# A fused attention and expert kernel: the order of steps inside a batch is changed

## The chip, the cores and the metric

The kernel runs on one core of a Trainium2 chip (trn2). The metric is the device time of one execution in microseconds (us), the median of the runs shown. The engines are called TensorE (PE), VectorE (DVE), ScalarE (ACT), GpSimd (POOL) and SyncE (SP); SP issues most of the DMAs here.

## The reference, cut to what matters

The input is 16 batches of 512 rows of 256 float32 numbers. Each row is normalised, and two branches of the normalised rows are added to the input.

```python
xn = layernorm(x)                                  # 16 x 512 x 256
x = x + attn(xn) + ffn(xn)

# attn: 16 heads of 16 columns, q and k through low-rank factors
q = (xn @ q_a) @ q_b;  k = (xn @ k_a) @ k_b;  v = xn @ v_w.T + v_b
att = softmax(where(causal, q k^T / sqrt(16), min))
y = (att @ v) @ o_w.T + o_b

# ffn: 8 experts, each takes the 128 rows of a batch with the highest probability
probs = softmax(xn @ choice_w.T)
G, I = top_k(probs transposed, 128)
out[I] += G * (silu(xn[I] @ w1) @ w2)
```

## The kernel before

The attention part comes first, and the experts after it. The change touches the attention part alone.

**Groups, slots and units.** A batch's 16 heads are worked on in four groups of four heads, so there are 64 groups, numbered n = 4 b + g. The attention part is a sequence of slots, one for each group: slot (b, g) has the number G = 4 b + g. A slot has ten units (`UN`). In every unit TensorE computes two tiles of 128 x 512 scores. The first, `scoret`, holds the transposed scores of group G + 1; ScalarE takes its exponential, and GpSimd sets the part above the diagonal to zero (L887, L565, L469). The second, `score`, holds the scores of group G + 3; VectorE takes its row maxima (L866, L719), which the later `scoret` of the same group subtracts. A `score` tile has three PSUM banks in turn, so the score of unit u waits until VectorE has finished that of unit u - 3; `scoret` has two banks, and waits for the exponential of unit u - 2.

**Steps between the units.** All other work is cut into steps, which `slot_steps` (L53) puts behind the units of a slot. Two tables by g say where: an entry (t, kind, ahead, k) stands behind unit t. `SUMS` holds the steps of a group: `pv` (probabilities times values, four steps; the last is followed by ScalarE's copy `yraw`), `maxt` and `maxd` (the row maxima are transposed, and written by a small DMA of ScalarE's queue into row KS of `qstk`), and `ytr` (transposing y back and dividing it by the denominator). `PROJECTIONS` holds the steps of a batch, for the batch b + ahead:

- `xload`: SP loads the rows of batch b + 2 into `xln` (L382). It waits only until the rows before it are normalised.
- `lnstat` (two halves), `lnapply`: VectorE takes mean and variance, GpSimd takes the power -1/2, VectorE writes `xn`, and SP stores it.
- `xt` (two): TensorE transposes `xn`, ScalarE and VectorE split it in a high and a low part.
- `qk_first` and `qk` (k = 0 to 3): three matmuls each of 128 x 512, the two halves of one tile of queries or keys. k = 0, 1 are queries, k = 2, 3 keys. ScalarE takes the high part (L537), and VectorE the rest (L588).
- `mid` (k = 0 to 3): ScalarE takes the middle part of a tile (L541), GpSimd the low one (L460). Behind k = 1 SP issues six DMAs of 256 KB that write the queries into `qstk`, and behind k = 3 six that write the keys into `kstk` (L393 to L400).
- `v` (four): the values and the router's logits of the next batch. `yt` (two), `o` (four): the output projection of the batch before. `xres`: loading of the input rows that the output is added to (L406), and GpSimd's addition of the bias (L477).

The first `score` of batch b + 1 stands in unit 0 of slot (b, 1), and waits for all twelve of those DMAs:

```python
if g == 0 and k == 0:
    pe.wait_ge(stacked[b % 2], at(STACK_DMAS * (b // 2 + 1), STACK_DMAS))
```

The keys of batch b + 1 are written behind `mid` k = 3 in slot (b, 0), the slot right before.

**What sets the order.** Every engine walks through the same list of steps and takes its own part of each, in the list's order, and SP its DMAs. The steps of the kinds in `shared` use two PSUM banks in turn, in the order of the list (`unit_of`). The whole order is thus the two tables. The 16 batches are run as eight pairs: the first and the last pair are written out, and pairs 1 to 6 are the body of a loop (`eng.Fori(1, PAIRS - 1)`, L342) which each engine runs by itself. Its back branch comes before the batches 4, 6, 8, 10 and 12. Those five are called the batches behind the branch here; 1, 2, 3, 5, 7, 9, 11, 13 and 14 are the nine others in whose slot 0 the keys of the next batch are written.

Of the kernel before, what the change touches and what calls it, by code (L numbers as in the profile page):

```python
# [25 lines left out]
def unit_parts(t, transposed):  # L26
# [5 lines left out]
    for h, i in parts:  # L32
# [4 lines left out]


PROJECTIONS = (
# [5 lines left out]
     (9, "qk_first", 2, 1)],  # L45
    [(0, "qk", 2, 1), (0, "mid", 2, 0), (1, "mid", 2, 1), (4, "qk_first", 2, 2), (6, "qk", 2, 2), (8, "mid", 2, 2),
     (8, "qk_first", 2, 3), (9, "qk", 2, 3)])

SUMS = (
# [4 lines left out]


def slot_steps(b, g):
# [1125 lines left out]
```

## Time and profile before

| what | value |
|---|---|
| median of 3 runs | 1301.05 us (1294.84 to 1301.11) |
| profiled execution, its own time | 1295.71 us |
| its span, first to last instruction | 1293.8 us |
| TensorE busy | 1184.1 us, 92% |
| VectorE busy | 967.2 us, 75% |
| ScalarE busy | 668.7 us, 52% |
| GpSimd busy | 692.0 us, 53% |

The page of the profile gives busy times by engine, the busy share in 40 slices of the span, and the costliest groups. Views of the trace give the same by stretch (windows), who waited for whom (waits), and the instructions of an engine in order of time (timeline). Times in them count from the start of the span. A matmul's duration in them covers its whole way through the array, so matmuls that follow each other overlap; what one costs is the distance to the next start.

### The profile page before, as it was taken

What the parts mean: (1) busy time and instruction counts of PE and PEld (TensorE: products, weight loads), DVE (VectorE), ACT (ScalarE), POOL (GpSimd) and SP (SyncE); (2) the same over time, 40 slices, a digit from 0 to 9 for tenths busy, and PEclk for the clock granted to TensorE, in tenths of its full rate; (3) what the DMA queues carried; (4) which work ended last, traced back from release to release, by engine and by line L of the source; (5) the groups of instructions that cost most, each with busy time, mean ns of one, the idle gap of its engine ahead of it and who ended that gap; (6) DMA issues with size and microseconds to landing.
All of it is one profiled execution on the core that took longest, in us unless ns stands there. A gap on an engine that the chain in (4) does not pass through costs nothing. (4 is left out here: it accounts for less than half of the span.)

```text
span 1293.8 us, 29459 instructions
## 1 busy us (share of the span) xinstructions
PE 1184.1 (92%) x8502; PEld 819.8 (63%) x8502; DVE 967.2 (75%) x3293; ACT 668.7 (52%) x1312; POOL 692.0 (53%) x1021
## 2 busy tenths in 40 slices
PE   6799999999999999999999998769999999999995
PEld 5545555555555555555555553348988888888885
DVE  3588888879889888888888879935666666666662
ACT  2357667667667677677667665522332323233320
POOL 1235344355355355345345443344888888888885
PEclk9779999999999999999999999979999999999998
DMA  5443443443443443443444342132555555556454
GB/s 141 114 116 83 116 116 100 116 116 98 115 115 98 115 115 99 115 115 100 113 115 112 100 99 67 34 114 38 111 99 95 114 93 102 94 100 109 85 78 53
DMA packets 106287, 130.31 MB, mean 101 GB/s; under 512 B 21580, under 2 KB 75476, under 8 KB 106196
## 3 DMA queue, kind: packets, MB, share of 16 engines
q1 hardware_dynamic: 76356, 94.46, 28.1%
q0 software_dynamic: 24576, 33.57, 15.6%
q10 hardware_dynamic: 5264, 1.32, 0.5%
q8 instruction: 27, 0.44, 0.1%
q14 instruction: 64, 0.52, 0.1%
HBM read 44.84 MB, written 33.55 MB: 61 GB/s over the span
## 5 line engine op out<-in xcount | busy, mean ns | idle before, releaser
L719 DVE CUSTOM_DVE_ANT_0 junk<-bank,rowmask 128x256 bf16<-128x256 f32 (+3 forms) x1024 | 454.9, 485 | 60.3 <-PE bank L866 38.0
L565 ACT ACTIVATE probs<-bank 128x512 f32<-128x512 f32 x640 | 377.3, 598 | 158.0 <-PE bank L887 143.8
L469 POOL TENSOR_SCALAR_AFFINE_SELECT probs<-probs 128x256 f32<-128x256 f32 (+1 forms) x640 | 224.2, 363 | 311.0 <-ACT probs L565 308.9
L866 PE MATMUL bank<-kstk,qstk 96*128 96x256 bf16 (+3 forms) x1024 | 250.7, 306 | 34.3 <-DVE rowmax L719 17.3
L887 PE MATMUL bank<-qstk,kstk 98*128 98x256 bf16 (+3 forms) x1024 | 251.0, 307 | 3.8 <-ACT probs L565 2.6
L1049 POOL DMA_INDIRECT out_rows<-mixed,rows x128 | 208.9, 1632 | 58.2 <-issue 38.1
L1078 ACT ACTIVATE hid<-bank 128x512 f32<-128x512 f32 x128 | 76.6, 598 | 228.5 <-PE bank L1141 228.5
L908 PE MATMUL bank<-probs,vaug 128*32 128x512 f32 (+3 forms) x2048 | 168.5, 448 | 6.6 <-POOL probs L469 6.6
L1157 PE MATMUL bank<-w_hi,hid_hi 128*128 128x256 f32 x512 | 147.3, 288 | 0.0
L1157 PE MATMUL bank<-w_hi,hid_lo 128*128 128x256 f32 x512 | 144.9, 283 | 0.0
L1157 PE MATMUL bank<-w_lo,hid_hi 128*128 128x256 f32 x512 | 144.8, 283 | 0.0
L866 PEld LDWEIGHTS bank<-kstk,qstk 96*128 96x128 bf16 x1024 | 89.7, 100 | 79.5 <-DVE rowmax L719 38.3
L887 PEld LDWEIGHTS bank<-qstk,kstk 98*128 98x128 bf16 x1024 | 76.7, 99 | 99.2 <-issue 48.0
L1109 DVE TENSOR_SCALAR mixed<-bank,gate_sel 128x256 f32<-128x256 f32 x128 | 56.1, 480 | 92.0 <-PE bank L1157 92.0
L908 PEld LDWEIGHTS bank<-probs,vaug 128*32 128x32 f32 x2048 | 54.1, 110 | 95.9 <-issue 74.1
L460 POOL TENSOR_TENSOR qk_part<-rest,qk_part 128x512 bf16<-128x512 f32 x64 | 74.6, 1166 | 58.0 <-ACT qk_part L541 55.1
L1157 PEld LDWEIGHTS bank<-w_lo,hid_hi 128*128 128x128 f32 x512 | 98.2, 192 | 0.0
L1157 PEld LDWEIGHTS bank<-w_hi,hid_hi 128*128 128x128 f32 x512 | 98.2, 192 | 0.0
L1157 PEld LDWEIGHTS bank<-w_hi,hid_lo 128*128 128x128 f32 x512 | 98.1, 192 | 0.0
L1098 DVE CAST hid_hi<-hid 128x512 fp32r<-128x512 f32 x128 | 56.9, 445 | 48.7 <-ACT hid L1078 47.1
L1100 DVE TENSOR_TENSOR hid_lo<-hid,hid_hi 128x512 fp32r<-128x512 f32 x128 | 89.2, 697 | 4.4
L719 DVE DVE_READ_ACCUMULATOR2_ANT rowmax<- 128x1 f32 x1024 | 84.8, 83 | 0.0
(131 smaller groups left out, 2097.8 us busy)
## 6 DMA issues: line engine op xcount, KB each, us to landing
qstk<-qk_part SPq DMA_DIRECT2D x96, 256.0 KB, 4.8
kstk<-qk_part SPq DMA_DIRECT2D x96, 256.0 KB, 4.7
xln<-in_L_attn_hidden_states SPq DMA_DIRECT2D x16, 512.0 KB, 6.1
xn_rows<-xn SPq DMA_DIRECT2D x16, 512.0 KB, 2.8
xres<-in_L_attn_hidden_states SPq DMA_DIRECT2D x16, 512.0 KB, 3.6
out_rows<-xres SPq DMA_DIRECT2D x16, 512.0 KB, 2.9
qstk<-in_L_ffn_w SPq DMA_DIRECT2D x8, 512.0 KB, 4.0
kstk<-in_L_ffn_w SPq DMA_DIRECT2D x8, 512.0 KB, 3.9
```

What stands on the lines that cost most here:

```text
L460: nc.gpsimd.tensor_tensor(qk_part[2][:, k, :], rest[k % 2][:], qk_part[1][:, k, :], ALU.subtract).then_inc(lo_done, 1)
L469: nc.gpsimd.affine_select(out=block, in_=block, compare_op=ALU.is_ge, fill=0.0, base=0, pattern=[[0, len(cols)], [1, P]], channel_multipli ...
L565: nc.scalar.activation(probs[n % 2][:, 512 * k:512 * k + 512], SCORET[k % 2][:], ACT.Exp, scale=SCALE).then_inc(exp_done, 1)
L719: last = nc.vector.tensor_tensor_reduce(out=junk[k % 2][:, col:col + width], in0=SCORE[score_bank(UN * n + k)][:, col:col + width], in1=ro ...
L866: last = nc.tensor.matmul(SCORE[score_bank(UN * n + k)][:, col:col + width], qstk[b % 2][0:KS, GH * g + h, P * i:P * i + P], kstk[b % 2][0 ...
L887: last = nc.tensor.matmul(SCORET[k % 2][:, col:col + width], kstk[b % 2][0:KS + SHIFT, GH * g + h, P * j:P * j + P], qstk[b % 2][0:KS + SH ...
L908: last = nc.tensor.matmul(Y[2 * HD * h:2 * HD * h + 2 * HD, P * k:T], vaug[b % 2][:, k, GH * g + h, :], probs[n % 2][:, col:col + width], ...
L1049: nc.gpsimd.indirect_dma_start(out=out_rows, out_offset=bass.IndirectOffsetOnAxis(ap=moe.rows[:, GB4 * grp + j, e:e + 1], axis=0), in_=mix ...
L1078: nc.scalar.activation(hid[k % 2][:], UP[k][:], ACT.Silu).then_inc(silu_done, 1)
L1098: nc.vector.tensor_copy(hid_hi[n % 2][:, k, :], hid[k % 2][:]).then_inc(hid_high, 1)
L1100: nc.vector.tensor_tensor(hid_lo[n % 2][:, k, :], hid[k % 2][:], hid_hi[n % 2][:, k, :], ALU.subtract).then_inc(hid_done, 1)
L1157: last = nc.tensor.matmul(DOWN[k][:, D * t:D * t + D], a, b, start=m == 0, stop=m == len(todo_mm) - 1)
```

## The change

The tables `PROJECTIONS` and `SUMS` are replaced, and nothing else. No step is added or removed. In `PROJECTIONS`, `xload` goes from unit 2 to unit 0 of slot 0; `lnstat` from (slot 0, unit 9) and (slot 1, unit 1) to units 5 and 9 of slot 0; `lnapply` from unit 5 to unit 2 of slot 1. `v` 0 leaves unit 0 of slot 0, and `v` 1, `v` 2 and `o` 0 stand in a group at unit 9 of slot 0; `v` 3 goes from unit 0 to unit 9 of slot 1. `yt` 0 goes from unit 1 to 0, `xres` from unit 1 to unit 9 of slot 2. `qk` 0, `qk_first` 1 and `qk` 1 stand in a group at unit 0 of slot 3; `mid` 0, 1 and 3 come one to two units later. In `SUMS`, `maxt`, `maxd`, `pv` 2 and `pv` 3 get places that differ by slot.

```diff
 PROJECTIONS = (
-    [(0, "v", 1, 0), (1, "mid", 1, 3), (1, "yt", -1, 0), (2, "xload", 2, 0), (6, "yt", -1, 1), (8, "v", 1, 1),
-     (9, "lnstat", 2, 0), (9, "v", 1, 2)],
-    [(0, "v", 1, 3), (1, "lnstat", 2, 1), (2, "o", -1, 0), (5, "lnapply", 2, 0), (5, "o", -1, 1), (6, "o", -1, 2),
-     (8, "o", -1, 3)],
-    [(0, "xt", 2, 0), (1, "xres", 0, 0), (1, "xt", 2, 1), (6, "qk_first", 2, 0), (8, "qk", 2, 0),
-     (9, "qk_first", 2, 1)],
-    [(0, "qk", 2, 1), (0, "mid", 2, 0), (1, "mid", 2, 1), (4, "qk_first", 2, 2), (6, "qk", 2, 2), (8, "mid", 2, 2),
-     (8, "qk_first", 2, 3), (9, "qk", 2, 3)])
+    [(0, "xload", 2, 0), (0, "yt", -1, 0), (2, "mid", 1, 3), (5, "lnstat", 2, 0), (6, "yt", -1, 1), (8, "v", 1, 0), (9, "v", 1, 1), (9, "v", 1, 2), (9, "lnstat", 2, 1), (9, "o", -1, 0)],
+    [(2, "lnapply", 2, 0), (6, "o", -1, 1), (6, "o", -1, 2), (8, "o", -1, 3), (9, "v", 1, 3)],
+    [(0, "xt", 2, 0), (1, "xt", 2, 1), (8, "qk_first", 2, 0), (9, "xres", 0, 0)],
+    [(0, "qk", 2, 0), (0, "qk_first", 2, 1), (0, "qk", 2, 1), (2, "mid", 2, 0), (3, "mid", 2, 1), (6, "qk_first", 2, 2), (8, "qk", 2, 2), (9, "mid", 2, 2), (9, "qk_first", 2, 3), (9, "qk", 2, 3)])

 SUMS = (
-    [(2, "pv", 0, 0), (2, "pv", 0, 1), (3, "maxt", 2, 0), (4, "maxd", 2, 0), (5, "pv", 0, 2), (5, "pv", 0, 3), (7, "ytr", 0, 0)],
...
+    [(2, "pv", 0, 0), (2, "pv", 0, 1), (4, "maxt", 2, 0), (5, "maxd", 2, 0), (5, "pv", 0, 2), (6, "pv", 0, 3), (7, "ytr", 0, 0)],
+    [(2, "pv", 0, 0), (2, "pv", 0, 1), (3, "pv", 0, 2), (3, "maxt", 2, 0), (4, "maxd", 2, 0), (5, "pv", 0, 3), (7, "ytr", 0, 0)],
+    [(2, "pv", 0, 0), (2, "pv", 0, 1), (2, "maxt", 2, 0), (2, "pv", 0, 2), (2, "maxd", 2, 0), (5, "pv", 0, 3), (7, "ytr", 0, 0)],
+    [(2, "pv", 0, 0), (2, "pv", 0, 1), (4, "maxt", 2, 0), (4, "pv", 0, 2), (5, "maxd", 2, 0), (5, "pv", 0, 3), (7, "ytr", 0, 0)])
```

The removed rows of `SUMS` are four times the one shown.

## Rows read from the trace of the kernel before

**Rows 1.** The page: TensorE's busy time, busy tenths, granted clock.

```profile
PE 1184.1 (92%) x8502; PEld 819.8 (63%) x8502; DVE 967.2 (75%) x3293; ACT 668.7 (52%) x1312; POOL 692.0 (53%) x1021
...
PE   6799999999999999999999998769999999999995
...
PEclk9779999999999999999999999979999999999998
```

**Rows 2.** Windows, slots of batches 7 and 8: length, then busy us by engine.

```profile
417.65:429.23 11.58, 11.46 (x97) 7.03 (x96) 10.08 (x40) 9.00 (x20) 4.77 (x12) 1.00 0.71 159
429.23:442.49 13.26, 11.75 (x101) 7.78 (x100) 10.90 (x50) 6.67 (x16) 4.75 (x12) 1.00 0.30 89
442.49:453.59 11.10, 11.02 (x89) 6.24 (x87) 10.14 (x42) 8.26 (x16) 4.02 (x6) 1.00 0.30 95
453.59:465.41 11.82, 11.74 (x85) 6.17 (x85) 9.88 (x40) 9.18 (x18) 8.35 (x19) 1.00 0.45 105
465.41:478.62 13.21, 11.80 (x96) 7.11 (x96) 9.81 (x40) 9.16 (x20) 4.77 (x12) 1.00 0.73 170
478.62:490.30 11.68, 11.68 (x101) 7.69 (x100) 10.77 (x50) 6.66 (x16) 4.71 (x12) 1.00 0.19 66
...
sum 95.65, PE 92.22 PEld 54.42 DVE 81.72 ACT 66.30 POOL 43.75; mean PE 11.53 PEld 6.80 DVE 10.22 ACT 8.29 POOL 5.47
```

**Rows 3.** Waits, whole span: us in total, times, longest.

```profile
PE bank L866 <- DVE rowmax L719: 17.3, 32, 1.3
...
DVE junk L719 <- issue: 15.2, 6, 3.0
...
PE bank L866 <- DMA kstk<-qk_part: 15.1, 9, 2.1
```

**Rows 4.** Timeline of TensorE around the slot change of batch 7.

```profile
428.38 0.39 PE L769 MATMUL bank<-wv_hi,xt_hi 128*128 128x264 f32 x1
...
429.23 0.39 PE L887 MATMUL bank<-qstk,kstk 98*128 98x512 bf16 x1
431.13 0.39 PE L866 MATMUL bank<-kstk,qstk 96*128 96x512 bf16 x1 [1.51 <-DMA kstk<-qk_part]
```

**Rows 5.** Timeline of ScalarE in batch 7, slot 0: its part of `mid` 3.

```profile
419.96 0.64 ACT L541 ACTIVATE qk_part<-rest 128x512 bf16<-128x512 f32 x1
```

**Rows 6.** Timeline of SP in 408 to 427 (start, us, line, tiles, count).

```profile
411.08 4.08 SPq L400 DMA_DIRECT2D qstk<-qk_part  x6
421.88 3.81 SPq L400 DMA_DIRECT2D kstk<-qk_part  x6
425.96 0.61 SPq L382 DMA_DIRECT2D xln<-in_L_attn_hidden_states  x1
```

**Rows 7.** Timeline of VectorE across the loop's branch, batch 8.

```profile
466.46 0.69 DVE L588 TENSOR_TENSOR rest<-bank,qk_part 128x512 f32<-128x512 f32 x1
470.13 0.69 DVE L719 CUSTOM_DVE_ANT_0 junk<-bank,rowmask 128x512 bf16<-128x512 f32 x1 [2.98 <-issue]
```

**Rows 8.** Timeline of TensorE in batch 8, slot 0: scores of units 3 and 5.

```profile
470.89 0.39 PE L866 MATMUL bank<-kstk,qstk 96*128 96x512 bf16 x1 [0.63 <-DVE rowmax L719]
...
472.87 0.39 PE L866 MATMUL bank<-kstk,qstk 96*128 96x512 bf16 x1 [0.66 <-DVE rowmax L719]
```

**Rows 9.** Timeline of TensorE: an `o` step and what follows it.

```profile
441.45 0.28 PE L769 MATMUL bank<-wo_lo,yt_hi 128*128 128x256 f32 x1
...
442.04 0.39 PE L887 MATMUL bank<-qstk,kstk 98*128 98x384 bf16 x2
```

**Rows 10.** The page, costliest groups: ScalarE's exponentials.

```profile
L565 ACT ACTIVATE probs<-bank 128x512 f32<-128x512 f32 x640 | 377.3, 598 | 158.0 <-PE bank L887 143.8
```

**Rows 11.** Line L400 in 421 to 426 (keys): issue to landing.

```profile
DMA to landing us min/median/max: 3.2/4.6/6.0
```

**Rows 12.** Line L400 in 410 to 416 (queries): issue to landing.

```profile
DMA to landing us min/median/max: 3.4/4.6/5.8
```

**Rows 13.** A window of VectorE's pause in batch 8 (last columns: clock, DMA share, GB/s).

```profile
467.50:469.70 2.20, 2.20 (x24) 0.90 (x22) 0.00 (x0) 1.84 (x4) 1.57 (x3) 1.00 0.01 6
```

3 rows, old and new, of the table SUMS are left out of this document.

## The prediction

> **What bounds the kernel now.** I read the page first: TensorE is busy 92% of the span, and in nearly every slice of the attention part the tenths say 9 or more at a granted clock of 9 tenths or more [rows 1]. Then one pair of batches by slots [rows 2]: TensorE is busy 92.22 of 95.65 us, VectorE 81.72, ScalarE 66.30. Every slot but two is TensorE's full time to within 0.12 us; the exceptions are slot 1 of batch 7 (13.26 long, 11.75 busy) and slot 0 of batch 8 (13.21 long, 11.80 busy). So the order of steps can give back only what TensorE idles, and the list of waits names both pieces [rows 3]: nine waits for the keys' DMAs, 15.1 us in all, and 17.3 us for VectorE's row maxima, which go with six pauses of VectorE that nothing releases (15.2 us, up to 3.0).
>
> *The keys.* In batch 7 TensorE issues the transposed score of slot 1 at 429.23, and the first score of the next batch only at 431.13 [rows 4], 1.90 later. The nine batches without the branch have this wait once each, and 15.1 / 9 = 1.68 of the 1.90 is the wait; the other 0.22 is the ordinary distance. The chain behind it, counted from the start of slot 0 at 417.65 [rows 2]: ScalarE's part of `mid` 3 at +2.31 [rows 5], GpSimd's behind it, SP's first issue at +4.23 [rows 6], the score at +13.48 [rows 4]. The DMAs alone are 9.25 us of that.
>
> *The branch.* In batch 8 VectorE issues the rest of `qk` 3 at 466.46 (+1.05 in the slot) and its next work at 470.13 (+4.72), idle for 2.98 us [rows 7]. TensorE meets this at the score of unit 3 (+5.48) and of unit 5 (+7.46) [rows 8]. The slot is 13.21 long where batch 7's takes 11.58 [rows 2], so 1.63 us are passed on. In return slot 1 of batch 8 doesn't wait for keys (11.68 against 13.26): the two losses cover each other, and a pair's two halves come out alike, 24.84 and 24.89 us for slots 0 and 1.
>
> **The change part by part.** No work is added, so TensorE's busy time stays, and only the two waits and new ones count.
>
> *o 0 into slot 0, v 0 and v 3 to the ends of their slots.* An `o` step costs 0.80 us (its last five matmuls take 442.04 - 441.45 = 0.59 [rows 9], the first some 0.2 more), a `v` 0.85 (428.38 to 429.23 [rows 4]). Slot 0 keeps its three `v` and gains `o` 0; slot 1 loses it. In a batch without the branch TensorE arrives at the first score of slot 1 at 11.58 + 0.23 + 0.80 = +12.6 instead of +11.8.
>
> *mid 3 from unit 1 to unit 2.* It now stands behind the exponential of unit 2 on ScalarE and the masking of unit 2 on GpSimd. With `v` 0 gone, ScalarE has one exponential of 0.60 [rows 10] more and the copies of `v` less in front of it, and must wait for unit 2's tile, which TensorE issues at about +1.4. I take +2.7 for ScalarE's part, 0.4 later than now, and the same 0.4 at SP: first issue at +4.63. Bounds: 0 (the `v` copies pay for it) and +1.2 (the whole distance of a unit, a tenth of 11.58). The keys then land for a score at 4.63 + 9.25 = +13.9, still behind TensorE's +12.6. So the wait stays at 1.3 us, and the slot change comes 0.4 later. What follows in slot 1 is 442.49 - 431.13 = 11.36 now and 10.56 without `o` 0. Slots 0 and 1: 13.9 + 10.56 = 24.4 against 24.84, a gain of 0.4 in each of nine batches.
>
> *xload to unit 0.* SP reaches it right behind the queries' DMAs, whose issue starts, with `mid` 1 two units later behind a group of three `qk` steps, some 8.5 us into slot 3, against 411.08 now. Rows and queries are then written by about +5.7 of slot 0, about when VectorE comes to `lnstat`, and before the keys' first packets. At present the load is issued behind the keys, at 425.96 [rows 6], and has nothing in front of it to gain from: the slowest DMA of the keys takes 6.0 us with the load behind it [rows 11], that of the queries 5.8 without [rows 12]. I count nothing for it; bounds: 0.2 us a batch won, and 2.4 lost if the rows, 512 KB, are still in front of the keys (256 KB take (9.25 - 3.2) / 5 = 1.2). The Trainium skill would allow more: "DMA: Bandwidth & Descriptors", "Issuing engines are not separate DMA queues", says that all DMAs run on the same 16 engines and interleave. By it the load could have slowed the keys, and its removal would give about a microsecond; the rows show 0.2.
>
> *The branch with v 0 gone.* VectorE is pinned: the rest of `qk` 3 still ends slot 3, so it restarts at +4.72, and what it does up to the score of unit 2 is the same. TensorE's score of unit 5 stays at +7.46 whatever TensorE does before, since it waits for unit 2's maxima. But `v` 0, which stood before that point, under the pause, now stands behind it, and so does `o` 0. From that score to the slot's end it is 478.62 - 472.87 = 5.75 us now, and 5.75 + 0.85 + 0.80 = 7.40 then, with 0.1 for `v` 0 waiting for a bank behind two more operations of VectorE (`lnstat` at unit 5): slot 0 takes 14.96 instead of 13.21, +1.75. Slot 1 loses `o` 0 (-0.80), and has three units without filler at its start, where the third transposed score waits for the first exponential: two units every 1.25 us by the 0.60 of an exponential [rows 10] and what I put around it, 0.35 more than the 0.90 of four tiles of 0.22. Slot 0 and 1: +1.3. Bounds: +0.8 (no new small wait, a fifth less passed on) and +2.3.
>
> *Slots 2 and 3.* `qk` 0, `qk_first` 1 move from slot 2 (11.10) to slot 3 (11.82) [rows 2], 1.5 us from one to the other and no change of their sum. Slot 2 falls to 9.6 us, for which VectorE has 10.14 - 0.69 = 9.45 us of work [rows 2, 7]: tight, but it carries up to two score tiles over. Small waits on VectorE go there (the list has 32, of 0.54 on average [rows 3]; I take 0.45 for the two slots), one of 0.35 for the exponential comes: -0.1. Bounds -0.5 and +0.8 (VectorE's deficit not carried). The pieces of `SUMS` move `pv` 2, `pv` 3 and `maxt` by a unit or two at the same cost; `xres`, eight units later, spares GpSimd a wait for its load, off the path.
>
> *The sum.* Nine batches x (-0.4 - 0.1) = -4.5. Five batches x (+1.3 - 0.1) = +6.0. Together +1.5 us: 1295.7 of the profiled execution becomes 1297.2. The median of the runs shown is 5.3 above that execution, and the same difference on it gives 1302.5; I put 1302.
>
> **The rivals.**
>
> 1. *The wait for the keys goes* (chance 0.28). If `mid` 3 is no later and TensorE's added 0.8 us fills the wait, nine batches win 0.8 + 0.1, with a shorter way of the keys up to the whole 1.67; with the branch at +0.6 in five: -9 x 1.3 + 5 x 0.6 = -8.7, 1292. For it: the way from ScalarE to SP has idle stretches. Against it: 9.25 of 13.48 us are DMAs that the change doesn't touch.
> 2. *VectorE's restart gets later* (chance 0.23), slower. The queries are issued 3 us later in slot 3 and the rows right behind them, so the DMA engines are at work while VectorE fetches what stands behind the branch; now they are nearly idle then, share 0.01 [rows 13]. The place is slot 0 of five batches, each us of the pause is passed on whole, and it decides from about 0.7 us on. With 1.5 us more, and the rows delaying the keys by 0.5 in nine batches: 5 x (1.2 + 1.5) + 9 x (-0.5 + 0.5) = +13.5, 1314. The Trainium skill speaks for the mechanism: "Runtime: NRT & Kernel Launch", "Instruction fetch mechanics", says that a taken branch outside the fetched window forces a DMA fetch before execution goes on. The trace's 2.98 us pause agrees.
> 3. *VectorE bounds slots 0 and 2* (chance 0.07): all of `lnstat` stands in slot 0 now, and slot 2 of 9.6 is shorter than VectorE's mean time in a slot, 81.72 / 8 = 10.2 [rows 2]. If nothing is carried over, 14 batches lose 0.6: 14 x 0.6 + 1.5 = +9.9, 1311.
>
> **How the numbers follow.** The forecast has the remaining chance, 0.42, with its own range of 1296 to 1308. A measurement of this kernel can tell 0.5%, 6.5 us, from no change. Faster by more than that: most of rival 1, and a little of the forecast, 0.27. Slower by more: rival 2 and most of 3, and the upper end of the branch's bound, 0.31. The rest, 0.42, is no change. The range reaches into rivals 1 and 2: 1288 to 1314.
>
> **What would show it.** The profile after should have slot 0 of a batch without the branch ending with `v`, `v`, `o` and then still a wait for the keys of about 1.3 us, SP's first key issue 4.6 us into the slot, and slots 0 and 1 together 24.4 us. Behind the branch slot 0 should take 15 us, VectorE's pause still 3.0, and slots 0 and 1 together 26.1. Slots 2 and 3 should be near 9.7 and 13.2. The forecast is wrong if the waits for the keys fall far below 9 x 1.3 us, if VectorE's pause changes, or if slot 2 is longer than 10.2.

## The result, and the profile after

| kernel | median | against before |
|---|---|---|
| before, beside it on the same chip | 1297.9 us (1293.5 to 1301.1) | |
| changed | 1321.6 us (1318.8 to 1323.4) | 1.018 [1.014, 1.023] |

The change makes the kernel slower by 1.8%, where the prediction said no change. The profiled execution of the changed kernel has a span of 1320.3 us, 26.5 more than before. Line numbers are four lower than before (L866 is L862, L887 L883, L719 L715, L400 L396, L382 L378).

The page of the changed kernel, its busy times, TensorE's busy tenths and the granted clock, to be held against [rows 1]:

```profile
PE 1191.3 (90%) x8502; PEld 822.0 (62%) x8502; DVE 1000.7 (76%) x3293; ACT 670.6 (51%) x1312; POOL 698.7 (53%) x1021
...
PE   6799999989989989989989997858999999999995
...
PEclk9779999989989989989989999978999999999998
```

Before, the nines ran through. Now an 8 comes back every three slices, some 100 us, the length of a loop pass, and the clock is 8 in the same slices. The windows of the slots of batches 7 and 8 in the changed kernel show where (columns as in [rows 2]; the third last is the clock):

```profile
426.72:439.55 12.83, 12.68 (x102) 7.71 (x102) 12.35 (x49) 9.88 (x23) 5.89 (x12) 1.00 0.94 215
439.55:450.78 11.23, 10.87 (x95) 6.75 (x94) 9.95 (x43) 6.52 (x12) 4.46 (x12) 1.00 0.14 48
450.78:460.56 9.78, 9.30 (x82) 5.33 (x81) 8.39 (x37) 7.04 (x16) 3.58 (x10) 1.00 0.32 108
460.56:474.09 13.53, 12.98 (x93) 7.32 (x91) 12.66 (x44) 9.84 (x19) 8.49 (x14) 1.00 0.28 69
474.09:495.36 21.27, 16.04 (x103) 9.12 (x102) 12.78 (x49) 10.05 (x23) 5.89 (x12) 0.76 0.54 131
495.36:506.24 10.88, 10.85 (x95) 6.69 (x94) 9.93 (x43) 6.51 (x12) 4.36 (x12) 1.00 0.14 49
```

One slot stands out: slot 0 of batch 8, the first behind the loop's back branch, takes 21.27 us where it took 13.21 [rows 2]. TensorE is idle for 5.2 of it, and its clock is 0.76 in the mean. Everything else is near the forecast.

From the starts of the batches (the distance from one batch's first transposed score to the next batch's) the difference of 26.5 us adds up:

| part | before | after | sum of the difference |
|---|---|---|---|
| five batches behind the branch | 47.8 to 47.9 | 54.8 to 55.9 | +37.0 |
| batches 7, 9, 11, 13 | 47.7 to 47.8 | 47.4 to 47.5 | -1.4 |
| batches 1, 2, 3, 5 | 48.2 to 50.0 | 47.4 to 47.7 | -6.5 |
| start, batches 0 and 14, all behind | | | -2.6 |

The waits of the whole span, to be held against [rows 3]:

```profile
PE bank L862 <- DVE rowmax L715: 41.6, 40, 5.0
...
DVE junk L715 <- issue: 28.8, 6, 5.8
...
PE bank L862 <- DMA kstk<-qk_part: 6.4, 10, 2.1
```

The wait for the keys fell from 15.1 to 6.4 us. But VectorE's pauses that nothing releases grew from 15.2 to 28.8 us, still six of them, and TensorE's waits for the row maxima from 17.3 to 41.6. The timeline of VectorE over the branch in batch 8, whose slot 0 starts at 474.09:

```profile
475.85 0.69 DVE L584 TENSOR_TENSOR rest<-bank,qk_part 128x512 f32<-128x512 f32 x1
482.23 0.69 DVE L715 CUSTOM_DVE_ANT_0 junk<-bank,rowmask 128x512 bf16<-128x512 f32 x1 [5.70 <-issue]
```

The rest of `qk` 3 is issued 1.76 us into the slot (before 1.05), the next work at +8.14 (before +4.72, [rows 7]): the pause is 5.70 us instead of 2.98. TensorE's score of unit 3 waits through it:

```profile
482.99 0.61 PE L862 MATMUL bank<-kstk,qstk 96*128 96x512 bf16 x1 [4.99 <-DVE rowmax L715]
...
485.44 0.63 PE L862 MATMUL bank<-kstk,qstk 96*128 96x512 bf16 x1
```

What SP issues around the branch, and what the DMA engines and the clock do then (timeline of SP; windows of 1 us with all engines):

```profile
469.18 3.80 SPq L396 DMA_DIRECT2D qstk<-qk_part  x6
473.78 0.39 SPq L378 DMA_DIRECT2D xln<-in_L_attn_hidden_states  x1
478.70 4.18 SPq L396 DMA_DIRECT2D kstk<-qk_part  x6
```

```profile
477.09:478.09 1.00, 0.91 (x9) 0.10 (x1) 0.00 (x0) 0.31 (x2) 0.89 (x2) 1.00 1.08 269
478.09:479.09 1.00, 0.00 (x0) 0.00 (x0) 0.00 (x0) 0.55 (x1) 0.87 (x2) 1.00 0.68 214
479.09:480.09 1.00, 0.00 (x0) 0.00 (x0) 0.00 (x0) 0.00 (x0) 0.01 (x1) 1.00 0.21 62
480.09:481.09 1.00, 0.00 (x0) 0.00 (x0) 0.00 (x0) 0.00 (x0) 0.00 (x0) 1.00 0.96 272
481.09:482.09 1.00, 0.00 (x0) 0.00 (x0) 0.00 (x0) 0.00 (x0) 0.00 (x0) 0.60 1.08 266
482.09:483.09 1.00, 0.10 (x1) 0.11 (x2) 0.86 (x3) 0.00 (x0) 0.00 (x0) 0.50 1.05 236
...
490.09:491.09 1.00, 1.00 (x7) 0.97 (x5) 0.74 (x2) 0.72 (x2) 0.12 (x1) 0.50 0.00 0
491.09:492.09 1.00, 1.00 (x7) 0.67 (x6) 0.88 (x6) 0.32 (x1) 0.29 (x1) 0.78 0.03 8
492.09:493.09 1.00, 1.00 (x10) 0.82 (x10) 0.96 (x3) 0.53 (x3) 0.29 (x1) 1.00 0.00 0
```

VectorE meets its branch at 475.94, and the queries and rows (2 MB in SP's queue) keep the DMA engines full until 478 and the last of them busy until 479.8, where before they were nearly idle [rows 13]. TensorE, with no `v` 0 to do, stands still for four whole windows; in the fourth of them its granted clock falls, and stays at 0.50, the lower of its two levels (1.2 GHz), until 491, 8 us after TensorE has work again.

One kind of packet tells when VectorE can go on. The DMA queue that the profile calls `instruction` carries one packet of 8 KB behind each of VectorE's branches. The DMA view of a window of 0.2 us around it, in the changed kernel (479.70 to 479.90, 3.84 us behind the branch) and in the one before (467.70 to 467.90, 1.2 us behind it):

```profile
q14 instruction: 1, 0.01, 9.7%
```

```profile
q14 instruction: 1, 0.01, 10.8%
```

In both, VectorE's next work starts 2.4 us after this packet, and in both the packet starts within 0.05 us of the last one of the queries and rows that stood queued. Few of the 16 DMA engines are still busy then. In the 0.9 us before it (478.90 to 479.78, changed kernel) the queries and rows fill 8.8% of the 16 engines, that is one or two of them; and an instruction packet at 473.60 starts while they are full (473.50 to 473.70):

```profile
q1 hardware_dynamic: 28, 0.03, 8.8%
```

```profile
q1 hardware_dynamic: 29, 0.05, 114.5%
q14 instruction: 1, 0.01, 18.9%
```

So the packet behind the branch seems to stand in line on one engine, the one that ends last.

### The profile page after: what moved, and what is told of

It reads as the page before. It is cut to its first block and busy times, and to the rows that moved or that the text cites. A ratio compares the mean times of both kernels' runs of the same rounds, so it can differ in the third digit from the quotient of the medians.

```text
span 1320.3 us, 29425 instructions
## 1 busy us (share of the span) xinstructions
PE 1191.3 (90%) x8502; PEld 822.0 (62%) x8502; DVE 1000.7 (76%) x3293; ACT 670.6 (51%) x1312; POOL 698.7 (53%) x1021
## 3 DMA queue, kind: packets, MB, share of 16 engines
q0 software_dynamic: 24576, 33.57, 15.1%
## 5 line engine op out<-in xcount | busy, mean ns | idle before, releaser
L715 DVE CUSTOM_DVE_ANT_0 junk<-bank,rowmask 128x256 bf16<-128x256 f32 (+3 forms) x1024 | 450.7, 485 | 78.5 <-PE bank L862 37.0
L561 ACT ACTIVATE probs<-bank 128x512 f32<-128x512 f32 x640 | 370.9, 599 | 175.0 <-PE bank L883 169.4
L465 POOL TENSOR_SCALAR_AFFINE_SELECT probs<-probs 128x256 f32<-128x256 f32 (+1 forms) x640 | 231.6, 364 | 402.0 <-ACT probs L561 396.1
L862 PE MATMUL bank<-kstk,qstk 96*128 96x256 bf16 (+3 forms) x1024 | 255.3, 311 | 49.0 <-DVE rowmax L715 41.6
L883 PE MATMUL bank<-qstk,kstk 98*128 98x256 bf16 (+3 forms) x1024 | 254.4, 311 | 10.5 <-ACT probs L561 8.8
L904 PE MATMUL bank<-probs,vaug 128*32 128x512 f32 (+3 forms) x2048 | 179.4, 451 | 1.3 <-POOL probs L465 1.3
L883 PEld LDWEIGHTS bank<-qstk,kstk 98*128 98x128 bf16 x1024 | 82.2, 99 | 133.7 <-issue 61.1
L862 PEld LDWEIGHTS bank<-kstk,qstk 96*128 96x128 bf16 x1024 | 89.3, 100 | 93.6 <-DVE rowmax L715 63.3
L904 PEld LDWEIGHTS bank<-probs,vaug 128*32 128x32 f32 x2048 | 49.9, 110 | 94.8 <-issue 90.3
L1137 PE MATMUL bank<-pt_hi,w_hi 128*128 128x512 f32 x256 | 81.6, 401 | 4.9 <-DVE pt_lo L1090 4.9
```

Of the source, the lines that this page charges most:

```text
L465: nc.gpsimd.affine_select(out=block, in_=block, compare_op=ALU.is_ge, fill=0.0, base=0, pattern=[[0, len(cols)], [1, P]], channel_multipli ...
L561: nc.scalar.activation(probs[n % 2][:, 512 * k:512 * k + 512], SCORET[k % 2][:], ACT.Exp, scale=SCALE).then_inc(exp_done, 1)
L715: last = nc.vector.tensor_tensor_reduce(out=junk[k % 2][:, col:col + width], in0=SCORE[score_bank(UN * n + k)][:, col:col + width], in1=ro ...
L862: last = nc.tensor.matmul(SCORE[score_bank(UN * n + k)][:, col:col + width], qstk[b % 2][0:KS, GH * g + h, P * i:P * i + P], kstk[b % 2][0 ...
L883: last = nc.tensor.matmul(SCORET[k % 2][:, col:col + width], kstk[b % 2][0:KS + SHIFT, GH * g + h, P * j:P * j + P], qstk[b % 2][0:KS + SH ...
L904: last = nc.tensor.matmul(Y[2 * HD * h:2 * HD * h + 2 * HD, P * k:T], vaug[b % 2][:, k, GH * g + h, :], probs[n % 2][:, col:col + width], ...
```

## The experiments

Each has its ratio to the kernel before, run on the same chip. "Branch slot" is slot 0 of the batches behind the branch, "fetch" the time from VectorE's branch to the instruction packet.

| run | us | ratio, 95% interval | branch slot | fetch |
|---|---|---|---|---|
| e1 changed, no loop | 1286.1 | 0.993 [0.991, 0.995] | 12.6 | |
| e2 before, no loop | 1301.9 | 1.006 [1.004, 1.008] | | |
| e3 changed, rows back | 1340.8 | 1.035 [1.033, 1.037] | 19.0 | 2.0 |
| e4 changed, queries back | 1330.9 | 1.028 [1.027, 1.030] | 15.1; 17.6, 18.7 | 1.0; 2.3 |
| e5 before, wait filled | 1290.2 | 0.996 [0.994, 0.999] | 14.8 | 1.2 |
| e6 before, rows early | 1306.7 | 1.009 [1.007, 1.012] | 16.9, the first 15.7 | 3.2, the first 2.6 |
| e7 changed, branch at slot 3 | 1315.3 | 1.015 [1.012, 1.018] | slot 3: 20.9 | 1.0 to 1.3 |
| e8 changed, no loop, filled | 1275.6 | 0.985 [0.983, 0.988] | 13.4 | |
| e9 changed, TensorE kept busy | 1314.3 | 1.015 [1.013, 1.018] | 18.6 | 3.85 |
| e10 before, filled, late statistics | 1319.6 | 1.020 [1.017, 1.022] | 14.8 to 16.4 | 1.2 |
| e11 changed, rows behind keys | 1340.4 | 1.036 [1.034, 1.038] | 18.1 to 19.1 | 2.0 |
| e12 e8 with `mid` 3 sooner | 1276.0 | 0.986 [0.984, 0.989] | 13.4 | |
| e13 e6, rows by ScalarE's queue | 1303.1 | 1.005 [1.003, 1.007] | 13.2 | 1.24 |
| e14 changed, rows by ScalarE's queue | 1320.5 | 1.019 [1.018, 1.021] | 20.3 to 20.7 | 3.8 |

**e1 and e2: without the loop's branch.** The changed order and the order of before, each with the six pairs of the loop written out; nothing is left out.

```diff
-                with eng.Fori(1, PAIRS - 1) as i:
-                    steps_fn(pair_steps(1), lambda value, per_pair: i * per_pair + (value - per_pair))
+                for i in range(1, PAIRS - 1):
+                    steps_fn(pair_steps(i), same)
```

> The changed order with the loop over pairs 1 to 6 written out, so that no engine takes a back branch in the attention part; the list of steps is the same. Theory A (the loss is VectorE's pause at the branch, 5.7 us with the DMA engines at work, and TensorE's idle time and lower clock that follow): slot 0 of batches 4, 6, 8, 10, 12 falls from 21 to the 12.8 of the other batches, 5 x 8 = 40 us, so about 1282 us, faster than before too. Rival B (the order itself overloads VectorE in slot 0, whatever the branch, or instructions come late from memory without a branch as well): 1310 us or more, and pauses of VectorE remain.

> The order before with the loop written out. VectorE's pause of 3.0 us goes in five batches, but the wait for the keys stood behind it in the same batches: slots 0 and 1 together stay at 24.8, the time within 2 us of before. Rival: the pause was a loss of its own, 5 x 1.6 = 8 us faster.

The changed order is then 0.7% faster than the kernel before, every batch from 1 to 13 takes 47.2 to 48.0 us, and VectorE has no pause over 0.5 us left. The waits of e1:

```profile
PE bank L862 <- DVE rowmax L715: 15.0, 30, 1.3
PE bank L862 <- DMA kstk<-qk_part: 14.8, 15, 2.4
```

So the whole loss sits in the branch, and by itself (e1 against e2) the new order is 16 us better than the old one. e2 itself gains nothing from losing the branch: without it the batches that had it wait for the keys like the others (25.7 us in 15 waits, where [rows 3] has nine). In the old order the pause and the wait for the keys covered each other, as the prediction said of it.

e2 is even 0.6% slower than the kernel before, and the windows show one reason. In the old order TensorE's clock falls behind some of the waits for the keys, and slot 1 then takes some 2 us longer, 1.5 of them more busy time for the same matmuls: 15.3 to 15.9 us at a mean clock of 0.89 in batches 1, 6, 11 and 13 of e2, and 15.4 and 14.9 in batches 1 and 5 of the kernel before, where the others take 13.3 at 1.00. Batch 5 of the kernel before, slot 1:

```profile
332.02:346.87 14.85, 13.31 (x102) 8.77 (x101) 11.23 (x50) 6.81 (x16) 4.79 (x12) 0.89 0.27 80
```

In e1 the clock stays at 1.00 from batch 1 to 13, so some 6 of its 16 us over e2 (4 x 1.5) are the clock. Why it falls in one batch and not in the next is not shown: the wait in batch 5 is 1.53 us, and in batch 7 1.51 [rows 4].

**e3 and e11: the rows back behind the keys.** The order of the queries stays late.

```diff
# e3: changed order, slots 0 and 1
-    [(0, "xload", 2, 0), ... (5, "lnstat", 2, 0), ... (9, "lnstat", 2, 1), (9, "o", -1, 0)],
-    [(2, "lnapply", 2, 0), ...
+    [..., (3, "xload", 2, 0), ... (9, "lnstat", 2, 0), ... (9, "o", -1, 0)],
+    [(1, "lnstat", 2, 1), (5, "lnapply", 2, 0), ...
# e11: the load as in e3, and in slot 1
+    [(3, "lnstat", 2, 0), (5, "lnstat", 2, 1), ... (8, "lnapply", 2, 0), ...
```

> The changed order with the steps of the rows (xload, lnstat, lnapply) back at about their places before: the load is issued behind the keys. Theory A1 (the instruction fetch waits for what SP has queued): one load of 1.2 us less is in front of it, VectorE's pause falls from 5.7 to about 4.5 us, and TensorE's idle time with it; with its clock kept more than 6 us faster than the changed kernel, to 1300 to 1315 us. Rival C (it is the queries' DMAs alone, issued late in slot 3, that the fetch meets): pause still 5.7, time unchanged at 1320.

> The changed order in its loop, with xload issued behind the keys as before, lnstat at units 3 and 5 and lnapply at unit 8 of slot 1. Theory A1: VectorE's first fetch packet comes 2.0 us after its branch instead of 3.8, slot 0 behind the branch falls from 21.2 to about 19 us, the other batches stay at 47.4: 1310 us. Rival (the early rows are worth their 2 us a batch also where VectorE doesn't wait for them): the other batches take 49 us or more, 1325.

The branch slot fell from 21.3 to 19, as e11 expected, with VectorE's pause at 3.8 (e3 had 4.5). The clock still falls behind the branch: its mean is 0.82 in slot 0 of batch 8. The totals missed by 25 us and more: the other batches rose from 47.4 to 49.7 (e3) and 49.4 (e11). In e3 VectorE waits for the rows:

```profile
DVE stats L653 <- DMA xln<-in_L_attn_hidden_states: 25.3, 9, 4.0
```

In e11, which gives the load all of slot 0 before the statistics, the lateness moved on to slots 1 and 2 (12.5 and 10.6 us against 11.3 and 9.8). The early rows are therefore worth 2 us a batch in this order, and cost 2.3 in each branch slot. The prediction had counted nothing for either.

**e4: the queries back.**

```diff
-    [(0, "xt", 2, 0), (1, "xt", 2, 1), (8, "qk_first", 2, 0), (9, "xres", 0, 0)],
-    [(0, "qk", 2, 0), (0, "qk_first", 2, 1), (0, "qk", 2, 1), (2, "mid", 2, 0), (3, "mid", 2, 1), ...
+    [(0, "xt", 2, 0), (1, "xt", 2, 1), (6, "qk_first", 2, 0), (8, "qk", 2, 0), (9, "qk_first", 2, 1), (9, "xres", 0, 0)],
+    [(0, "qk", 2, 1), (0, "mid", 2, 0), (1, "mid", 2, 1), ...
```

> The changed order with the qk units, mid 0, 1 and 2 back at their places before, so that the queries' DMAs are issued 5.4 instead of 9 us into slot 3; the load of the rows still comes right behind them. Theory A1: the queue is empty about 2 us earlier at the branch, pause 4 us, TensorE idles under 3 us and keeps its clock: 1300 to 1306 us. Rival D (the load of the rows alone delays the fetch, wherever it stands): pause still over 5 us, 1315 or more.

Where the DMA engines had drained at the branch, in batches 4, 6 and 12, the slot took 15.06 to 15.11 us, which is the prediction's 14.96 to 0.15 us. In batches 8 and 10 they hadn't: the fetch came at 2.3, the clock fell (mean 0.90 and 0.82), and the slot took 17.6 and 18.7. The total missed because slots 2 and 3 took 24.9 us instead of 23.3, with a new wait for the exponentials (27.9 us in 33 waits on L883), and 26.5 in batches 2, 3, 5 and 11, where the clock fell in slot 3. Slot 3 of batches 5 and 7:

```profile
365.11:380.29 15.18, 13.67 (x86) 6.57 (x85) 11.47 (x40) 9.21 (x18) 9.11 (x14) 0.89 0.50 115
466.61:480.35 13.74, 12.23 (x86) 6.08 (x85) 11.56 (x40) 9.14 (x18) 9.21 (x15) 1.00 0.44 104
```

The engines had drained just behind those longer slots 3 (of batches 3, 5 and 11), so the cheap branch slots were paid for with 1.4 us one slot earlier.

**e6, e13 and e14: the rows alone, and by another queue.** e6 is the kernel before with nothing moved but `xload`, from unit 2 to unit 0 of slot 0. e13 is e6, and e14 the changed kernel, with that load issued by ScalarE at the same place of the list:

```diff
# SP
-                        if kind == "xload":
+                        if kind == "xload" and n < 2:
# ScalarE
+                        if kind == "xload" and n >= 2:
+                            act.wait_ge(xn_done, at(n, 2))
+                            act.sem_inc(act_past, 1)
+                            act.dma_start(xln[:], x_v[at(n, 2)]).then_inc(x_in, 16)
```

> The order before, with xload alone moved to unit 0 of slot 0, so that the load of the rows is issued right behind the queries' DMAs. Theory A1 (the instruction fetch comes behind what SP has queued): the first fetch packet after VectorE's branch comes about 1 us later (2.2 instead of 1.24 us), the pause grows from 3.0 to 4 us, and the wait for the keys behind it hides most: time within 4 us of before. Rival D (the load of the rows is what the fetch can't pass): pause over 5.5 us and 15 us slower or more.

> The kernel before with the rows' load at unit 0 of slot 0, as in e6, but issued by ScalarE's queue instead of SP's (for batches 2 and later). Theory Q (the instruction fetch behind VectorE's branch waits for packets that stand in SP's queue): with only the queries' tail in SP's queue, as in the kernel before, the fetch packet comes 1.2 to 1.5 us behind the branch, the next work 3.6 to 3.9, slot 0 of a branch batch takes 13.2 to 13.5 and the kernel is within 4 us of the kernel before. Rival E (the fetch waits for the 16 DMA engines, whoever queued the packets): the rows are issued at the same time by another queue, so the fetch packet comes about 3.2 us behind the branch and slot 0 takes 16 to 17, as in e6; some 12 us over the kernel before. ScalarE's issue of 0.6 us itself costs at most 0.5 us a batch.

> The changed kernel with the rows' load issued by ScalarE's queue (batches 2 and later), at the same place in the order. Theory Q: SP's queue holds the queries alone at the branch, as in e3, so the fetch packet comes 2.0 us behind it instead of 3.84, VectorE's next work at 4.4 instead of 6.3, slot 0 of a branch batch takes 18 to 19 instead of 21.3, and the kernel about 1309 where the changed one takes 1321.6. Rival E: the fetch waits for the DMA engines, 3.8 us and 21.3 as in the changed kernel, 1320 to 1323.

e6 costs 12 us by one DMA moved, where 4 had been expected: the fetch comes at 3.2 instead of 1.24 (expected 2.2), and the branch slots take 16.9 at a clock of 0.80 in the mean. VectorE's wait for the rows goes (20.8 us before, 0.7 now), but batches 7, 9, 11 and 13 win only 0.15 us each. Its longest pause:

```profile
472.55 0.69 DVE L715 CUSTOM_DVE_ANT_0 junk<-bank,rowmask 128x512 bf16<-128x512 f32 x1 [4.93 <-issue]
```

e13 brings slot 0 back to 13.2 and the fetch to 1.24, the numbers of theory Q (the total does not come with them: it is 7 us over the kernel before, beyond the 4 allowed, since slots 0 and 1 take 25.2 us instead of 24.8, and 26.8 in four batches where the clock fell in slot 1). But the timeline shows why it doesn't speak for Q: ScalarE comes to the load later than SP, 0.70 us behind VectorE's branch at 468.46, and the first packets of the rows start behind the fetch.

```profile
469.16 0.40 ACTq L503 DMA_DIRECT2D xln<-in_L_attn_hidden_states  x1
```

e14 decides. There the load is issued 0.83 us ahead of the branch at 474.09, the queue of SP has drained by +2.2, and the fetch still comes only at +3.91 (478.00), with the last packet of ScalarE's queue, to 0.02 us. The DMA view of 476.5 to 477.9, and of 477.9 to 478.1:

```profile
q10 hardware_dynamic: 166, 0.15, 35.5%
```

```profile
q14 instruction: 1, 0.01, 9.7%
q10 hardware_dynamic: 3, 0.00, 3.2%
```

All five branches show the same (3.78 to 3.91, each with the last packet of that queue). Rival E holds: the fetch waits for packets queued ahead of it on the DMA engines, whichever engine issued them. What e13 adds is that 512 KB issued 0.7 us behind the branch don't delay VectorE. Slot 0 of batch 8 is 0.6 us shorter than in the changed kernel with nearly the same pause; its mean clock is 0.83, and 0.76 in the changed kernel.

**e9: TensorE kept busy in the pause.** The changed kernel with 22 more matmuls ahead of the transposed score k = 3 in slot 0 of the loop's even batches (2 to 12); their results are overwritten. That is 4.8 us of added work at full clock in each of these slots.

```diff
+                            for _ in range(22 if (n, k) == (9, 3) else 0):
+                                nc.tensor.matmul(SCORET[k % 2][:], kstk[b % 2][0:KS + SHIFT, GH * g, 0:P],
+                                                 qstk[b % 2][0:KS + SHIFT, GH * g, 0:T], start=True, stop=True)
```

> The changed kernel with 22 matmuls of 98 x 512 more in slot 0 of the loop's even batches (2 to 12), in front of the transposed score of unit 3, into the bank that it overwrites: extra work of 4.8 us that fills TensorE's idle time in VectorE's pause and changes no result. Theory A2 (of the 8.5 us that slot 0 loses behind the branch, the pause explains some 5.6 and TensorE's lower clock after its idle stretch the rest): the granted clock stays at 1.00, slot 0 falls from 21.2 to 18.4 us in five batches, batch 2 gets 4.8 us longer: 1320 - 5 x 2.9 + 4.8 = 1310 us. Rival E (the half clock has another cause than the idle stretch, or costs nothing because VectorE bounds the slot then): slot 0 stays at 21 us and the kernel gets slower, 1325 us.

With 4.8 us more to compute in six slots, the kernel is not slower: 1314.3 us, ratio 1.015, beside 1321.6, ratio 1.018. By the two ratios, each against the kernel before on the same chip, the totals can't be told apart (1310 had been expected); the slots can. The pause of VectorE is the same (5.8), the fetch too; the windows of e9 show the clock:

```profile
473.52:492.05 18.53, 17.58 (x125) 9.82 (x124) 12.44 (x49) 9.97 (x23) 5.90 (x12) 1.00 0.62 150
```

The branch slot is 2.7 us shorter (18.6 against 21.3) at a clock of 1.00 against 0.76. Batch 2, which has the added work but no branch, pays 4.5 us for it (17.38 against 12.84). So 2.7 us of the branch slot are TensorE's clock.

**e7: the branch elsewhere.** The changed order with the loop's body turned to begin at slot 3 of the even batches; four back branches instead of five.

```diff
+                head = lambda i: [s for g in range(3) for s in slot_steps(2 * i, g)]
+                tail = lambda i: pair_steps(i)[len(head(i)):]
-                steps_fn(prologue_steps() + pair_steps(0), same)
+                steps_fn(prologue_steps() + pair_steps(0) + head(1), same)
...
```

> The changed order, step for step, in a loop whose body begins at slot 3 of the even batch, where SP has nothing queued and three qk steps, 2.4 us of TensorE's work, stand behind the first unit; four back branches instead of five. Theory A: VectorE's pause is 3 us or less, TensorE hardly idles and keeps its clock, slot 0 is 12.8 us in all batches: 1320 - 5 x 8 + 4 x 0.5 = 1282 us. Rival B (the branch costs what it costs, wherever it stands): 4 x 7 us remain, 1308 us.

Slot 0 is 12.8 in every batch, as forecast, but slot 3 behind the branch takes 20.9 instead of 13.5, though the DMA engines have next to nothing queued there (fetch at 1.0 to 1.3). The clock falls here too, to 0.84 in the mean of the slot of batch 8. Two engines pause there, one behind the other. The timelines of ScalarE and of VectorE:

```profile
510.62 0.60 ACT L563 ACTIVATE probs<-bank 128x512 f32<-128x512 f32 x1 [2.29 <-issue]
```

```profile
514.88 0.69 DVE L717 CUSTOM_DVE_ANT_0 junk<-bank,rowmask 128x512 bf16<-128x512 f32 x1 [3.40 <-issue]
```

Slot 3 has little slack for either: VectorE is busy for 12.66 of its 13.53 us in batch 7 of the changed kernel. The expected 1282 was missed; a quiet DMA queue alone doesn't make a branch cheap.

**e5 and e10: the order of before with its wait for the keys filled.** e5 puts `v` 3 and `o` 0 behind unit 9 of slot 0, ahead of the first score that needs the keys. e10 also takes the statistics back, since e5 showed VectorE waiting for the rows.

```diff
# e5, slots 0 and 1 of the order of before
-     (9, "lnstat", 2, 0), (9, "v", 1, 2)],
-    [(0, "v", 1, 3), (1, "lnstat", 2, 1), (2, "o", -1, 0), (5, "lnapply", 2, 0), ...
+     (9, "lnstat", 2, 0), (9, "v", 1, 2), (9, "v", 1, 3), (9, "o", -1, 0)],
+    [(1, "lnstat", 2, 1), (5, "lnapply", 2, 0), ...
# e10
+     (9, "v", 1, 2), (9, "v", 1, 3), (9, "o", -1, 0)],
+    [(3, "lnstat", 2, 0), (5, "lnstat", 2, 1), ... (8, "lnapply", 2, 0)],
```

> The order before, with v 3 and o 0 taken from slot 1 to the end of slot 0, so that 1.65 us of TensorE's work stand in front of the wait for the keys; mid 3, the rows and the queries stay where they were. Theory A: the wait of 1.68 us in nine batches is filled (slots 0 and 1 together 24.84 to about 23.3), and behind the branch nothing changes, since VectorE's pause is still 3 us: 9 x 1.5 = 13 us faster, 1282 us beside a before of 1295. Rival: slot 1 gets three units in a row without filler and loses what was won, within 3 us of before.

> The order before, in its loop, with v 3 and o 0 at the end of slot 0 and VectorE's lnstat at units 3 and 5 and lnapply at unit 8 of slot 1, so that VectorE doesn't stand waiting for the rows in front of the scores of slot 1. Theory A: what the filled kernel lost again in slot 1 (11.55 us where 9.9 is its work) was that wait of VectorE's, 1.5 us a batch; slots 0 and 1 together fall to 23.3 in nine batches, 1281 to 1284 us. Rival: slot 1 is bound by something else (its three units without filler), within 2 us of the filled kernel, 1290.

In e5 the keys' wait is gone (three left, 3.5 us), yet slots 0 and 1 of the other batches only fall from 24.84 to 24.7: the row maxima wait in VectorE behind statistics that wait for the rows. In e10 these slots take 23.8, and slot 2 12.8 instead of 11.1, since TensorE's transposes now wait for `xn`. Where the clock falls in addition, slot 2 takes 14.5 (batches 1, 3, 9 and 13; mean 0.88 in batch 9) and the branch slot 15.9 to 16.4 instead of 14.8 (0.90 in batch 8, 1.00 in batch 6). The waits of e5 and of e10:

```profile
DVE stats L653 <- DMA xln<-in_L_attn_hidden_states: 21.5, 14, 2.9
```

```profile
PE bank L841 <- DVE xn L668: 25.8, 15, 2.2
```

Both missed, and together they say what the early `xload` is for: load, statistics, `xn` and transposes are a chain of their own, right behind the keys' in length. Filling one wait without moving the other gives 0.1 us.

**e8 and e12: the best version.** e1 (changed order, loop written out) with `v` 3 moved from slot 1 to unit 9 of slot 0, and e12 with `mid` 3 back at unit 1 as well.

```diff
-... (9, "v", 1, 2), (9, "lnstat", 2, 1), (9, "o", -1, 0)],
-    [(2, "lnapply", 2, 0), ... (8, "o", -1, 3), (9, "v", 1, 3)],
+... (9, "v", 1, 2), (9, "v", 1, 3), (9, "lnstat", 2, 1), (9, "o", -1, 0)],
+    [(2, "lnapply", 2, 0), ... (8, "o", -1, 3)],
# e12 also
-... (2, "mid", 1, 3), ...
+... (1, "mid", 1, 3), ...
```

> The changed order with the loop written out and v 3 taken from slot 1 to slot 0, in front of what is left of the wait for the keys (14.8 us in 15 waits). Theory A: slots 0 and 1 together fall from 24.5 by 0.5 to 0.8 us in 14 batches, 1276 us beside an unrolled 1286. Rival: the keys' DMAs land when they land and the rest of slot 1 has no slack, so the two kernels are within 2 us.

> The unrolled, filled kernel with mid 3 back at unit 1 of slot 0. Theory A: the keys' DMAs are issued 0.3 to 0.4 us sooner, and the 6.4 us of waits for them that are left nearly go: 1272 to 1275 us beside 1275.6. Rival (mid 3 in front of unit 2's exponential delays ScalarE's tiles by as much): no difference beyond 1 us.

e8 takes 1275.6 us, 1.5% less than the kernel before and, by the two ratios, 3.3% less than the changed one; most of its batches take 46.5 to 47.1 us. Its waits for the keys fell from e1's 14.8 us to

```profile
PE bank L862 <- DMA kstk<-qk_part: 6.4, 9, 2.0
```

e12 halves them again (3.4 us) and gains nothing, as its rival had it, so the keys are no longer what the slots wait for last: the 15.8 us for the row maxima are still there.

## Why the prediction was wrong, by its own steps

**The step that failed: "VectorE is pinned ... so it restarts at +4.72", in the branch's term.** VectorE restarts at +8.14. The term of +1.3 us (with slots 2 and 3: +1.2) for each of five batches was +7.4 on average (37.0 / 5). From e3, e4, e9 and the trace after it splits into:

- 1.75 us, `v` 0 and `o` 0 behind the pause instead of under it, as the prediction had it; e4's 15.06 us in the slots with a drained queue comes within 0.15 us of the 14.96.
- 3.4 us, the later restart: 2.6 of them the fetch packet, held back until queries and rows had left the DMA engines (3.84 against 1.2), the rest the later rest of `qk` 3 (+0.7).
- some 2.9 us, what is left, and mostly TensorE's clock: its 5 us of idleness took it to the lower level. e9 gives back 2.7 of them.

That makes 8.1 us in slot 0 of batch 8. Slot 1 gave 0.8 back (10.88 against 11.68) and slots 2 and 3 took 0.4, and the first of the five batches lost less (6.9).

**Rival 2 was the right mechanism and was priced too low.** It named the place, the cause (queries and rows in the DMA engines while VectorE fetches) and the side. It put 1.5 us on the later restart instead of 3.4, and did not see that a longer stop of TensorE also costs its clock, so it ended at 1314 and not at 1322. The size was at hand: by the forecast's own times the rows would be written at +5.7 of the slot, some 4.5 us behind the branch. That number stood in the prediction, next to a pause taken as unchanged. It came to +6.3 (the last of the rows landed at 480.43, the slot began at 474.09).

**Slots 0 and 1 of the other batches: right in direction, better in size.** Forecast 24.4, measured 24.1 (24.84 before). SP's first key issue was put at +4.63 and came at +4.5 to +4.6. In batch 7 the keys let the first score go at +13.58 instead of +13.9, and TensorE came to it 0.4 us before: slot 0 took 12.83 instead of the 12.4 to which its terms add up. So the wait is 0.4 us, not the 1.3 that "stays". (The 1.3 was also read a little high: it rests on the mean of nine waits, 1.68, where batch 7's own is 1.51 [rows 4].) Rival 1 was half true here, at a gain too small to see beside the branch.

**Slots 2 and 3.** Forecast 9.7 and 13.2, measured 9.78 and 13.51. That is 0.37 us more for the two than before instead of 0.1 less; in the sum of a batch it cancels the point above (-0.35 measured, -0.5 forecast). Rival 3 did not come: slot 2 is not over 10.2.

**The early rows "count for nothing".** Right for the slots of batches 7, 9, 11 and 13 in the order of before (e6: -0.15 us a batch), wrong for the new one: e3 and e11 show 2 us a batch. With the keys' wait shortened, the rows' chain is the next in length.

**Batches 1, 2, 3 and 5** took 48.2 to 50.0 us before and were counted like the others at -0.5; they gave 1.6 each. In batches 1 and 5 some 1.5 us of that was the clock in slot 1 (0.89 in the mean), which the changed order keeps at 1.00. The prediction read one pair, batches 7 and 8, in which the clock was 1.00 throughout, and multiplied.

## What to carry to other kernels

A loop's back branch is a place in the schedule: look which engine has a pause behind it, what the DMA engines still have queued at that moment, and what work the waiting engine has to cover it, before moving any of the three. A transfer that is moved sooner is not free because nothing waits for the engines' bandwidth; an instruction fetch may stand behind it, whichever queue issued it. When a filled wait gives nothing, ask which chain was just as long, and move both; and price a new idle stretch of TensorE with the clock it may lose behind it. When equal slots differ by 1.5 us or so from batch to batch, look at the granted clock before looking for another cause.

## What the runs showed of the hardware

- Behind VectorE's back branch an 8 KB packet of the instruction queue starts when the last queued data packet has ended: 1.2, 2.0, 3.2 and 3.8 us behind the branch in batch 8 (before, e3, e6, changed), within 0.05 us each; in e14 behind packets of another engine's queue. With nothing queued any more (first branch of the kernel before, e7, and batches 4, 6 and 12 of e4) the packet comes at 1.0, in one case of e7 at 1.3. (In e7 and in batches 6 and 12 of e4 another 8 KB packet comes sooner, at 0.1 to 0.7. The one at 1.0 is taken as VectorE's because its next work comes 2.2 to 2.5 us after it, as in every other run; the profile does not name the engine.) So 3.3 to 3.5 us are the floor of a branch here. At 1.2 the kernel before was thus nearly at the floor.
- The packet starts when the engine that ends last is done: in the 0.6 us before it a mean of 1.1 to 1.2 of the 16 DMA engines is busy (before, e3, e6, changed, e14), and other instruction packets start amid full queues (473.60 in the changed kernel). That the fetch is tied to one engine fits both; it was not tried by itself.
- With the loop where it is, only VectorE pauses; ScalarE and GpSimd go on 0.4 and 1.1 to 1.5 us behind their own branches. With the loop begun at slot 3 (e7) ScalarE pauses too (2.3 us), with VectorE's 3.4 behind it. What decides which engine pauses stays open.
- TensorE's granted clock fell to 0.50 in the stop of 5 us behind the branch (last matmul issued at 477.61, the fall in 481.09 to 482.09), and was back at 1.00 by 492, at a cost of 2.7 us (e9). In the kernel before, whose idle pieces behind the branch are below 0.7 us [rows 8], it stayed at 1.00 [rows 2]. But it also fell right behind waits for the keys of 2.1 and 1.5 us (slot 1 of batches 1 and 5 of the kernel before, mean 0.89), and not in the one of 1.5 us in batch 7; behind which waits it falls stays open.
